# x brought to tokens by VectorE block transposes and DRAM instead of TensorE transposes

## The reference

```
xn = layernorm(x)
proj = xn @ in_proj_w.T ; gate, xBC, dt = split(proj)
xBC = silu(causal_conv4(xBC)) ; x, B, C = split(xBC)      # x: 128 heads of 64 channels
xdt = x * dt                                              # per token and head
Ydiag = (C B^T * Lmat) xdt          # inside a chunk of 128 tokens
states = B^T (decay * xdt) ; scan over the 4 chunks ; Yoff = C prev_state * exp(cs)
y = Ydiag + Yoff + x * D ; out = rmsnorm_group(y * silu(gate)) * norm_w @ out_proj_w.T
result = x_in + out * silu(ffn(xn))
```

## Time and profile before

| | |
|---|---|
| median of 3 runs | 1763.05 us (1760.43 to 1763.21) |
| the profiled execution | 1765.14 us, its span 1763.3 us |
| PE busy | 1744.2 us, 99% |
| DVE busy | 1403.1 us, 80% |
| ACT busy | 1222.0 us, 69% |
| POOL busy | 1233.2 us, 70% |
| mean granted TensorE clock | 0.999 of full speed |
| DMA engines busy, q1 | 34.6% |

### The profile page before, as it was taken

How to read it: one execution, slowest core, us unless ns; L and a number is a source line. 1 busy time by engine, 2 the same in 40 slices (tenths; PEclk the granted TensorE clock), 3 DMA queues, 4 the chain that set the end, 5 groups by cost and what they waited for, 6 DMA issues and landing times.

```text
span 1763.3 us, 30295 instructions
## 1 busy us (share of the span) xinstructions
PE 1744.2 (99%) x10297; PEld 1460.6 (83%) x10297; DVE 1403.1 (80%) x2211; ACT 1222.0 (69%) x2456; POOL 1233.2 (70%) x877
## 2 busy tenths in 40 slices
PE   8999999999999999999999999999999999999999
PEld 6788888888888888888888888888888888888877
DVE  7878788878788788778788788878887887868941
ACT  6987678777777777777877777767777777643320
POOL 5677787777777787678776787677777777676630
PEclk9999999999999999999999999999999999999999
DMA  5433333233423333333333332334323343235522
GB/s 196 159 129 102 118 102 123 91 129 109 129 92 106 108 130 111 107 99 121 118 102 117 116 117 101 102 108 131 118 92 101 111 131 105 78 97 170 149 78 96
DMA packets 122595, 202.84 MB, mean 115 GB/s; under 512 B 23056, under 2 KB 60560, under 8 KB 122192
## 3 DMA queue, kind: packets, MB, share of 16 engines
q1 hardware_dynamic: 120720, 197.32, 34.6%
q10 hardware_dynamic: 1728, 3.65, 0.5%
HBM read 193.57 MB, written 7.34 MB: 114 GB/s over the span
## 4 chain that ended last, share of the span: by engine, by line
PE 88%; DVE 4%; issue 2%; POOL 2%; ACT 2%; DMA 2%; SPq 0%; ACTq 0%; DVEq 0%; POOLq 0%
PE bank L142 16%; PE bank L144 15%; PE bank L143 15%; PE bank L572 9%; PE bank L608 6%; PE bank L676 6%; PE bank L678 6%; PE bank L677 6%; PE bank L884 3%; PE bank L737 3%; DMA raw_g<-w_conv_dram 1%; DVE acc L1333 0%; POOL yt L1590 0%; ACT lm L960 0%; PE bank L699 0%
## 5 line engine op out<-in xcount | busy, mean ns | idle before, releaser
L960 ACT ACTIVATE lm<-lm,hp 128x128 f32<-128x128 f32 x1024 | 313.0, 389 | 0.8
L1242 DVE SCALAR_TENSOR_TENSOR z<-bank,cw_all,z 128x511 f32<-128x511 f32 (+2 forms) x384 | 286.6, 746 | 10.5 <-ACT z L996 1.4
L1607 POOL TENSOR_TENSOR conv_lo<-raw_x,conv_hi 128x512 fp32r<-128x512 f32 x124 | 203.0, 1637 | 121.6 <-ACT conv_hi L897 121.4
L142 PE MATMUL bank<-xn_hi,conv_hi 128*128 128x512 f32 x640 | 262.2, 410 | 5.1 <-DVE b_t L1242 2.3
L1302 DVE TENSOR_TENSOR xdt<-bank,hp 128x512 f32<-128x512 f32 x128 | 88.2, 689 | 212.8 <-PE bank L737 212.8
L1590 POOL TENSOR_TENSOR yt<-yt,ec 128x384 f32<-128x384 f32 x128 | 147.9, 1156 | 149.0 <-DVE ec L1311 117.6
L144 PE MATMUL bank<-xn_hi,conv_lo 128*128 128x512 f32 x640 | 251.2, 393 | 0.0
L143 PE MATMUL bank<-xn_lo,conv_hi 128*128 128x512 f32 x640 | 250.1, 391 | 0.0
L1276 DVE SCALAR_TENSOR_TENSOR lm<-lm,gm 128x1024 f32<-128x1024 f32 x128 | 223.8, 1748 | 12.9 <-ACT lm L960 12.9
L142 PE MATMUL bank<-xn_hi,gate_hi 128*128 128x512 f32 x512 | 213.1, 416 | 0.0
L1574 POOL TENSOR_TENSOR y_lo<-yt,y_hi 128x512 fp32r<-128x512 f32 x128 | 177.5, 1386 | 50.4 <-ACT y_hi L1031 50.4
(11 more groups left out here) (150 smaller groups left out, 4049.7 us busy)
## 6 DMA issues: line engine op xcount, KB each, us to landing
lm<-cs_d SPq DMA_DIRECT2D x128, 512.0 KB, 4.4
raw_x<-w_conv_dram SPq DMA_DIRECT2D x128, 256.0 KB, 3.4
ec<-e_d SPq DMA_DIRECT2D x256, 96.0 KB, 2.7
raw_o<-w_out_dram SPq DMA_DIRECT2D x64, 256.0 KB, 3.0
raw_g<-w_gate_dram SPq DMA_DIRECT2D x61, 256.0 KB, 3.0
raw_g<-w_conv_dram SPq DMA_DIRECT2D x16, 256.0 KB, 3.5
raw_o<-w_conv_dram SPq DMA_DIRECT2D x14, 256.0 KB, 3.4
q_raw<-w1q_dram SPq DMA_DIRECT2D x10, 256.0 KB, 3.8
```

The lines of the kernel that those rows point to most:

```text
L142: pe.matmul(dst, a_hi, b_hi, start=(i == 0), stop=False)
L960: e = act.activation(lm[m % LM_BUFS][:, u, :], lm[m % LM_BUFS][:, u, :], ACT.Exp, bias=hp[bd.seq][:, Q_CS, k1, u:u + 1])
L1242: dve.scalar_tensor_tensor(dst[:, d:SEQ], src[:, 0:SEQ - d], cw_all[:, bd.group, pos, 3 - d:4 - d], dst[:, d:SEQ], ALU.mult, ALU.add).then ...
L1607: pool.tensor_tensor(conv_lo[kx % 2][:, :, :], raw_x[:, kx % 2, :].rearrange("p (k j) -> p k j", k=KT), conv_hi[kx % 2][:, :, :].bitcast(F ...
```

## The change

For tiles 8 to 123 (`by_dma`, 116 tiles) TensorE no longer transposes x. Instead, for tile t = n+1, in step n:

- VectorE, after its `ec` product, transposes `xt` in 32x32 blocks into `blocks`, which is the second slot of `raw_x`.
- SyncE, as the first thing of step n, waits for that (`blk_done`) and writes `blocks` to a DRAM tensor `xb_d` (256 KB, 2 KB a partition).
- SyncE, as the last thing of step n, waits for that write (`xb_out`) and for the `diag` that used the `xdt` slot two tiles before, and reads it back in four DMAs of 32 partitions, in runs of 32 numbers (128 bytes), so that the 32x32 blocks come to their places in `xdt`.
- VectorE, as the first thing of step n+1, waits for the four (`xtok_in`), makes `xw` first, and then `xdt` in place.

As `raw_x` has one slot left for the weights, its load for tile n+5 now stands after the `ec` loads and waits for GpSimd's L1607 of the same step. TensorE's two products into `ps_x` get a wait on `st_done` that the transposes carried before. `paired` reaches to tile 123, the B/C piece of the second sequence's successor moves from k = 2 to k = 3, and two wide products into `ps_y` are put into the start-up.

The diff, without its declarations of names:

```diff
@@ -108,7 +109,12 @@
 
 def paired(n):
 
-    return TILES // 2 <= n < TILES * (BODIES - 1)
+    return TILES // 2 <= n < TILES * (BODIES - 1) + TILES // 2
+
+
+def by_dma(t):
+
+    return paired(t - 1) and paired(t) and t >= TILES
 
 
 def group_exists(group):
@@ -133,7 +139,8 @@
 def bc_piece(body, k):
 
     nx = body.plus(1)
-    return [(nx, k // 2 - 1)] if k in (2, 4) and nx.exists() else []
+    first = 3 if nx.seq else 2
+    return [(nx, 1 if k == 4 else 0)] if k in (first, 4) and nx.exists() else []
 
 
 def split_mm(pe, dst, terms):
@@ -386,6 +397,20 @@
                 return lm[3][:, 0:NC, :].rearrange("p c l -> p (c l)")
             return raw_g[:, :] if body.seq else raw_o[:, :]
 
+        blocks = raw_x[:, 1, :]
+
+        def dma_tiles(t):
+
+            return sum(1 for u in range(t + 1) if by_dma(u))
+
+        def x_slot(m):
+
+            return raw_x[:, m % 2 if m <= TILES + 1 else 0, :]
+
+        def xtok_count(t):
+
+            return 16 * BLK * sum(1 for u in range(t % 2, t + 1, 2) if by_dma(u))
+
         def sq_tile(kp):
 
             return sq_sum[:, :] if kp == 0 else gate[:, kp % 4, :]
@@ -432,12 +457,17 @@
 
             def step(body, k):
 
+                t = TILES * body.n + k + 1
+                if by_dma(t):
+                    sp.wait_ge(blk_done, dma_tiles(t))
+                    wait(sp, xtok_in[t % 2], xtok_count(t - 2))
+                    sp.dma_start(xb_d[t % 2].rearrange("g i c b j -> (g i) (c b j)"), blocks).then_inc(xb_out, 16)
                 bx, kx = at(body, k, 5)
-                if bx.exists():
-
+                mx = TILES * bx.n + kx
+                if bx.exists() and mx <= TILES + 1:
                     if kx > 0:
-                        wait(sp, wlo_x, TILES * bx.n + kx - 1)
-                    sp.dma_start(raw_x[:, kx % 2, :], w_conv[bx.group, X_POS[kx]]).then_inc(rawx_in[kx % 2], 16)
+                        wait(sp, wlo_x, mx - 1)
+                    sp.dma_start(x_slot(mx), w_conv[bx.group, X_POS[kx]]).then_inc(rawx_in[kx % 2], 16)
                 nx = body.plus(1)
                 if k == 3 and nx.exists() and body.n > 0:
                     load_hp(nx)
@@ -452,6 +482,9 @@
                         sp.dma_start(ec[ke % 2][HD * j:HD * j + HD, :],
                                      e_d[bd.seq, GH * bd.group + 2 * ke + j, CHUNK:SEQ].partition_broadcast(HD)
                                      ).then_inc(ec_in[ke % 2], 16)
+                if bx.exists() and mx > TILES + 1:
+                    sp.wait_ge(wlo_x, mx)
+                    sp.dma_start(x_slot(mx), w_conv[bx.group, X_POS[kx]]).then_inc(rawx_in[kx % 2], 16)
                 bd, k1 = at(body, k, 1)
                 for group, pos in out_piece(bd, k1):
                     wait(sp, wlo_o, TILES * group + pos)
@@ -472,6 +505,14 @@
                     else:
                         sp.wait_ge(wlo_o, TILES * body.group + TILES)
                     sp.dma_start(bc_raw(nb), w_conv[nb.group, BC_POS[i]]).then_inc(rawb_in, 16)
+                if by_dma(t):
+                    sp.wait_ge(xb_out, 16 * dma_tiles(t))
+                    sp.wait_ge(yd_done, t - 1)
+                    for b in range(BLK):
+                        o = slice(32 * b, 32 * b + 32)
+                        sp.dma_start(xdt[t % 2][o, :].rearrange("i (c g j) -> i c g j", c=NC, g=BLK),
+                                     xb_d[t % 2, :, :, :, b].rearrange("g i c j -> i c g j")
+                                     ).then_inc(xtok_in[t % 2], 16)
                 if k == 4 and body.is_number(0):
 
                     sp.wait_ge(hp_out, 16 * SEQS)
@@ -615,6 +656,7 @@
                 pe.wait_ge(t0_done, n)
                 diag(n - 1, ps_y)
                 pe.wait_ge(xw_done, n + 1)
+                pe.wait_ge(st_done, n)
                 diag(n, ps_x)
 
             def y_diag(body, k):
@@ -631,6 +673,7 @@
                 n = TILES * body.n + k
                 if body.exists():
                     pe.wait_ge(xw_done, n + 1)
+                    wait(pe, st_done, n)
                     if paired(n) and k % 2:
                         pe.wait_ge(y1_done, n + 1)
                     if k == 0:
@@ -730,7 +773,7 @@
             def turn_x(body, k):
                 n = TILES * body.n + k
                 bd, k1 = at(body, k, 1)
-                if bd.exists():
+                if bd.exists() and not by_dma(n + 1):
                     pe.wait_ge(xs_done, TILES * bd.n + k1 + 1)
                     wait(pe, st_done, n + 1)
                     for c in range(NC):
@@ -827,6 +870,9 @@
             for j in range(2):
                 mm = pe.matmul(ps_x[:, HD * j:HD * j + HD], d_row[:, :], pick[:, j, :], start=True, stop=True)
             mm.then_inc(dmm_done, 1)
+            for _ in range(2):
+                pe.matmul(ps_y[:, :].rearrange("p (r j) -> p r j", r=NC), ident[:, :],
+                          ident[:, :].unsqueeze(1).broadcast_to((P, NC, P)), start=True, stop=True)
             extra(FILL, 4)
             conv(FILL, 6)
             pe.wait_ge(xnlo_done, TT)
@@ -894,7 +940,7 @@
                     m = TILES * bd.n + kx
                     act.wait_ge(rawx_in[kx % 2], 16 * (TILES // 2 * bd.n + kx // 2 + 1))
                     wait(act, xp_done, m - 1)
-                    act.activation(conv_hi[kx % 2][:, :, :], raw_x[:, kx % 2, :].rearrange("p (k j) -> p k j", k=KT),
+                    act.activation(conv_hi[kx % 2][:, :, :], x_slot(m).rearrange("p (k j) -> p k j", k=KT),
                                    ACT.Copy).then_inc(whi_x, 1)
 
             def raw_bc(body, k):
@@ -1295,21 +1341,41 @@
 
                 if body.exists():
 
-                    dve.wait_ge(tx_done, n + 1)
+                    if by_dma(n):
+                        dve.wait_ge(xtok_in[n % 2], xtok_count(n))
+                    else:
+                        dve.wait_ge(tx_done, n + 1 - dma_tiles(n))
                     if k == 0:
                         wait_hp(dve, body)
+                    x_tok = xdt[n % 2] if by_dma(n) else ps_x
+
+                    def weighted():
+                        wait(dve, st_mm, n)
+                        dve.tensor_tensor(by_head(xw[:, :]), by_head(x_tok[:, 0:(NC - 1) * P]),
+                                          per_token(hp[body.seq], Q_DEC, k, NC - 1), ALU.mult).then_inc(xw_done, 1)
+
+                    if by_dma(n):
+                        weighted()
+                        dve.wait_ge(xw_done, n + 1)
                     wait(dve, yd_done, n - 1)
-                    dve.tensor_tensor(by_head(xdt[n % 2][:, :]), by_head(ps_x[:, :]),
+                    dve.tensor_tensor(by_head(xdt[n % 2][:, :]), by_head(x_tok[:, :]),
                                       per_token(hp[body.seq], Q_DT, k, NC), ALU.mult).then_inc(xdt_done, 1)
-                    wait(dve, st_mm, n)
-                    dve.tensor_tensor(by_head(xw[:, :]), by_head(ps_x[:, 0:(NC - 1) * P]),
-                                      per_token(hp[body.seq], Q_DEC, k, NC - 1), ALU.mult).then_inc(xw_done, 1)
+                    if not by_dma(n):
+                        weighted()
                 if pv.exists():
 
                     dve.wait_ge(yo_done, n)
                     dve.wait_ge(ec_in[kp % 2], 32 * (TILES // 2 * pv.n + kp // 2 + 1))
                     dve.tensor_tensor(ec[kp % 2][:, :], ps_y[:, P:NC * P], ec[kp % 2][:, :], ALU.mult
                                       ).then_inc(t0_done, 1)
+
+                if by_dma(n + 1):
+                    dve.wait_ge(xs_done, n + 2)
+                    if by_dma(n):
+                        dve.wait_ge(xb_out, 16 * dma_tiles(n))
+                    else:
+                        dve.wait_ge(wlo_x, TILES + 2)
+                    dve.transpose(blocks, xt[:, (k + 1) % 4, :]).then_inc(blk_done, 1)
 
                 if k == 0 and body.exists():
 
@@ -1605,7 +1671,7 @@
                 if bd.exists():
                     pool.wait_ge(whi_x, TILES * bd.n + kx + 1)
                     pool.tensor_tensor(conv_lo[kx % 2][:, :, :],
-                                       raw_x[:, kx % 2, :].rearrange("p (k j) -> p k j", k=KT),
+                                       x_slot(TILES * bd.n + kx).rearrange("p (k j) -> p k j", k=KT),
                                        conv_hi[kx % 2][:, :, :].bitcast(F32), ALU.subtract).then_inc(wlo_x, 1)
                 if paired(n) and k == 0:
                     sum_sq()
```

More of the change, by code:

```diff
@@ L49 @@
 LM_BUFS = 4
+BLK = P // 32
 SH = 4
@@ L165, in build @@
     hp_d = nc.dram_tensor("hp_d", (SEQS, P, NQ, GROUPS, TILES, 2 * NC), F32).ap()
+    xb_d = nc.dram_tensor("xb_d", (2, BLK, 32, NC, BLK, 32), F32).ap()
     mamba_d = nc.dram_tensor("mamba_d", (TT, P, DIM), F32).ap()
@@ L315, in build @@
         tx_done = sem("tx_done")
+        blk_done = sem("blk_done")
+        xb_out = sem("xb_out")
+        xtok_in = [sem(f"xtok_in{i}") for i in range(2)]
         xdt_done, xw_done = sem("xdt_done"), sem("xw_done")
```

## The result

The changed kernel takes 2086.35 us in the median of four runs (2081.31 to 2091.53); the kernel before took 1762.01 us on the same chip (1760.43 to 1763.21). The ratio is 1.1843 [1.1828, 1.1857]: 18.4% slower, 324 us. The profiled execution took 2091.53 us with a span of 2089.7.

A forecast was written before the change was run, and what follows sets the result against it. TensorE bound the kernel at 12.0 us a step; the new chain makes it 9.75 + 5.2 = 14.95, over 116 steps 341 us more. 1765.1 + 341 - 1.6 = 2104.5, about 2105 us (75%), range 1870 to 2370.

The forecast's parts named there:

- The new chain: From VectorE's first product with x (T) through GpSimd, SyncE's waits and the reads to the next T; closes whatever TensorE's speed.
- Even steps, T + 9.7: In even steps SyncE can issue the reads 9.7 us after T, VectorE's first product with x; 9.2 up to 10.3.
- Odd steps, T + 9.8: In odd steps SyncE can issue the reads 9.8 us after T, block transpose and early `diag` taken to cancel.
- The four reads, 5.2 us: Reads into `xdt`: fourth issued 1.7 us after the first, landing 3.5 later, 5.2 us; bounds 4.3 and 6.5.
- The sum, 14.95 a step: Step from T to T: 9.75 + 5.2 = 14.95 us in place of 12.0, over 116 steps 341 us more.
- 28 ns a packet, queue at 0.6: DMA engines: 28 ns a packet, 3.6 us for 2048 on 16 engines; queue share from 0.33 to about 0.6.
- The packets' rival: A 128-byte read packet costs as much as one of 2 KB, 83 ns: step 22.2 us, time 2950; chance 5%.
- `xdt` and `xw` at nothing: VectorE's two products reading SBUF in place of PSUM were taken to cost nothing more.
- TensorE near 80% busy: Sign in the profile after: TensorE busy near 80% of a longer span; over 95% would mean the clock.
- The rival that it falls: TensorE's clock falls from idling; with half its work at the low level, 16.6 us a step, 2300 us; chance 10%.
- The start-up, 1.6 us: Two wide products where TensorE idles in the start-up keep its clock up; up to 1.6 us won, all taken.
- The rival "faster": Chain fits under TensorE's 11.6 us a step, so 51 and 1.6 us are won: 1712 us; chance 6%.

## Why the prediction was right

Forecast 2105, measured 2086: the mechanism was the one foretold, and the size came out within 1%, partly as errors cancel. By its own steps:

- *The new chain.* Right, and shown by moving the reads: 290 of the 324 us are their place in SyncE's order.
- *Even steps, T + 9.7.* Measured 9.47. In the even step shown, GpSimd's L1673 takes 2.28 us where 1.3 is its usual time, beside VectorE's product of `lm` (L1322, 713.03 to 715.35); the even step before the change has such a stretched instruction too (L1590, 1.92 us). So part of the ring may be the same waiting for the port, and no run here takes it out.
- *Odd steps, T + 9.8.* Measured 10.58. I let the block transpose ahead of `inner` cancel against TensorE's early `diag`. It doesn't: the doubled transpose adds its 0.7 us to just these steps. With it 9.8 becomes 10.5.
- *The four reads, 5.2 us.* Measured 4.90. I took 0.56 us an issue and 3.5 for the landing; they are 0.636 and 2.9, and 3 * 0.636 + 2.9 = 4.8. The loads of `hp` gave the issue too low and the landing too high.
- *The sum, 14.95 a step.* Measured 14.93 (14.87 over all): +0.28 in the place of the reads and -0.30 in the handover, so the sum is right by errors that cancel. With the 12.03 of the same tiles before, 115 * (14.87 - 12.03) is 326 us, and the profiled executions differ by as much (2091.5 and 1765.1): nothing outside these steps has changed the time. The forecast's 341 has its 15 us too many from 14.95 and 12.0 in place of 14.87 and 12.03.
- *28 ns a packet, queue at 0.6.* Too high. The 0.6 adds the reads to a share of 0.33 that belongs to steps of 12.0 us; in steps of 14.95 it is 0.26, and the sum 0.5. The queue took 0.445 of the span, 0.346 before; (0.445 * 2089.7 - 0.346 * 1763.3) * 16 us over the 261,696 more packets are 19.5 ns each, the larger packets of the writes among them. Nothing hung on it. The packets' rival is refuted: it had 83 ns and 2950 us.
- *VectorE's 0.69 us.* 0.702 measured.
- *`xdt` and `xw` at nothing.* Wrong as a step, and small here. They are 802 and 597 ns in the mean (689 and 546 before), beside a VectorE that waits for the reads for 3.6 us a step; as both stand ahead of `ec`, at most 0.16 us a step of it can be in the ring. Once the reads are early it is the term that decides.
- *TensorE near 80% busy.* It is 86%. The work of a step is 840.99 / 67.0 = 12.6 us and not 11.55, with the clock at 0.93. The rival that it falls was right in its premise and wrong in its extent: half of the work at the low level would have made 16.6, and 12.6 is still under 14.9.
- *The start-up, 1.6 us.* The clock stays high, and the end isn't measurably earlier. No run bears out the 1.6.
- *It decides at 11.6.* The rival "faster" asked only whether the chain fits under TensorE's time. With early reads it does (5.9 + 4.9 = 10.8), and the kernel is still slower than before: the length of VectorE's products, once two of them read SBUF alone, was a condition that no rival had.

## What to carry to other kernels

A DMA round trip for data of the next step should be placed by what it needs, not at the end of the issuing engine's list: behind in-order waits for other engines it closes a ring, and no busy share shows it; count from an event of step n to the same event of step n+1. When work goes from a full engine to one with slack, look at where its operands will lie: two products on VectorE that were cheap from PSUM were not from SBUF beside a busy GpSimd. And when the long wait is gone, do the sum again, since an edit that helped under one bound (four writes in place of four reads, -86 us) hurt under the next (+35 us).

## What the runs showed of the hardware

- With early reads, VectorE's product of two SBUF operands (128x384) took 544 to 1685 ns beside GpSimd, from PSUM 540 to 560 in this run and the one that moved the operand, and GpSimd's own instruction was stretched in turn (2.28 us in place of 1.3). A slow group can be a group that waits inside its instruction.
- A DMA of 512 packets of 128 bytes costs SyncE 0.64 us to issue (median), one with the same bytes in rows of 2 KB 0.42, the write of 128 rows 0.33. The DMA engines needed some 19.5 ns a packet (an estimate from the queue's share before and after).
- The read of x back from DRAM as 256 KB in one DMA landed in 4.0 to 4.4 us (median; the weight loads of that size took 3.6 to 4.5 in the same two kernels), four of 64 KB issued one after the other in 2.9 each: four issues and a landing (4.9) cost only 0.8 us more than the one large read (4.1).
Over the whole kernel TensorE's products waited 47 times for `ec`, 2.6 us each in the mean, and the mean granted clock between 500 and 1500 us was 0.93.
